# The delta rule of a four-layer kernel in chunks of 128 tokens instead of 64

## What is computed

```python
C = 64                                        # chunk; N = 512 // C chunks
dec = cumsum(decay, within each chunk)
L_mask = exp(where(lower, dec_i - dec_j, -inf))
M = strict_lower(wk_beta @ wk.T * L_mask)
A = solve_triangular(eye(C) + M, eye(C))      # inverse of a unit lower triangle
v, wk_cumdecay = A @ v, A @ (wk_beta * exp(dec))
def step(S, chunk):                           # over the chunks, in order
    v_new = v_i - wkcd_i @ S
    o_i = (rk_i * exp(dec_i)) @ S + lower(rk_i @ wk_i.T * L_i) @ v_new
    S = S * exp(dec_i[-1]) + (wk_i * exp(dec_i[-1] - dec_i)).T @ v_new
```

## Time and profile before

| | before |
|---|---|
| median of 3 runs | 4818.0 us |
| span of the profiled execution | 4823.4 us |
| PE busy (matmul) | 4293.7 us, 89% |
| PE weight loads | 3431.0 us, 71% |
| DVE busy | 3207.6 us, 67% |
| ACT busy | 2619.0 us, 54% |
| POOL busy | 2413.5 us, 50% |

### The profile page before, as it was taken

The page is one execution under the profiler, slowest core; times in us unless marked ns, Lnnn a source line. Parts: engine busy times, 40 slices in busy tenths (PEclk is TensorE's granted clock), DMA queues, the critical chain, the costliest instruction groups (busy, mean ns, idle before and its releaser), DMA issues. The chain is left out here.

```text
span 4823.4 us, 167277 instructions
## 1 busy us (share of the span) xinstructions
PE 4293.7 (89%) x70890; PEld 3431.0 (71%) x70890; DVE 3207.6 (67%) x5446; ACT 2619.0 (54%) x4310; POOL 2413.5 (50%) x1965
## 2 busy tenths in 40 slices
PE   6997999999999999999999999999997768568767
PEld 5885777777777777777777777777774558457556
DVE  4445777777777777777778777777774553563553
ACT  2232566666566666566665666665664435445544
POOL 2123665566665656555656556566551255225034
PEclk9777999999999999999999999999998868768877
DMA  0000322222222222222222222232220111221022
GB/s 25 0 0 30 91 65 64 68 81 69 63 71 80 68 66 67 63 81 72 65 64 80 71 67 64 63 79 64 68 67 18 59 26 40 54 67 45 16 72 66
DMA packets 214409, 281.74 MB, mean 58 GB/s; under 512 B 59070, under 2 KB 103908, under 8 KB 212932
## 3 DMA queue, kind: packets, MB, share of 16 engines
q1 hardware_dynamic: 199940, 249.75, 19.5%
q0 software_dynamic: 9536, 19.55, 1.5%
q10 hardware_dynamic: 4224, 2.10, 0.2%
HBM read 54.88 MB, written 18.28 MB: 15 GB/s over the span
## 5 line engine op out<-in xcount | busy, mean ns | idle before, releaser
L1696 POOL TENSOR_TENSOR local_normed<-local_rot,local_sines 128x512 f32<-128x512 f32 x768 | 953.7, 1276 | 810.6 <-PE local_bank L1421 806.1
L1706 POOL TENSOR_TENSOR local_normed<-local_normed,local_inv_norm 128x1024 f32<-128x1024 f32 x384 | 733.1, 1930 | 278.3 <-ACT local_inv_norm L1596 278.3
L1773 DVE TENSOR_TENSOR local_rot<-local_bank,local_table 128x1024 f32<-128x1024 f32 x384 | 470.3, 1225 | 404.0 <-ACT local_squares L1577 397.4
L1341 PE MATMUL local_bank<-local_wqkv_hi,local_ys_hi 128*128 128x512 f32 x1152 | 494.8, 430 | 28.9 <-issue 17.4
L1572 ACT COPY local_v_tile<-local_bank 128x1024 f32<-128x1024 f32 x192 | 195.0, 1016 | 541.4 <-PE local_bank L1343 541.4
L1773 DVE TENSOR_TENSOR local_sines<-local_bank,local_table 128x1024 f32<-128x1024 f32 x384 | 466.4, 1215 | 0.0
L1779 DVE TENSOR_REDUCE local_norm<-local_squares 128x16 f32<-128x1024 f32 x384 | 464.1, 1209 | 0.0
L1343 PE MATMUL local_bank<-local_wqkv_hi,local_ys_lo 128*128 128x512 f32 x1152 | 458.1, 398 | 0.0
L1342 PE MATMUL local_bank<-local_wqkv_lo,local_ys_hi 128*128 128x512 f32 x1152 | 455.6, 395 | 0.0
L1577 ACT ACTIVATE local_squares<-local_bank 128x1024 f32<-128x1024 f32 x384 | 396.6, 1033 | 77.9 <-PE local_bank L1343 77.9
L1760 DVE TENSOR_REDUCE local_top<-local_bank 128x16 f32<-128x1024 f32 x192 | 234.8, 1223 | 244.9 <-PE local_bank L1369 244.5
(11 more groups left out here) (408 smaller groups left out, 9101.1 us busy)
## 6 DMA issues: line engine op xcount, KB each, us to landing
local_vals<-local_v_tile SPq DMA_DIRECT2D x1152, 130.0 KB
local_vals<-local_v_tile SPq DMA_DIRECT2D x672, 65.0 KB
local_stage<-in_L_ffn_Wqkv SPq DMA_DIRECT2D x6, 1536.0 KB
moe_w<-in_L_ffn_W SPq DMA_DIRECT2D x3, 2048.0 KB, 9.9
x_rows<-moe_rows SPq DMA_DIRECT2D x24, 256.0 KB, 4.9
moe_w<-y_rows SPq DMA_DIRECT2D x24, 256.0 KB, 5.5
local_wo<-in_L_ffn_Wo SPq DMA_DIRECT2D x6, 512.0 KB
moe_taken<-x_rows,moe_take POOLq DMA_INDIRECT x149
```

Of the source, the lines that this page charges most:

```text
L1341: nc.tensor.matmul(out, hi, wqkv_hi[:, d0:d1], start=True, stop=False)
L1696: last = nc.gpsimd.tensor_tensor(of_heads(normed, a)[:, :, to], of_heads(rot, a)[:, :, to], of_heads(sines, a)[:, :, of], ALU.add)
L1706: nc.gpsimd.tensor_tensor(of_heads(normed, a), of_heads(normed, a), inv_norm[:, a * HEADS:(a + 1) * HEADS].unsqueeze(2).to_broadcast([P, H ...
L1773: last = nc.vector.tensor_tensor(of_heads(out, a), src, table[:, m % TILES, row, :].unsqueeze(1).to_broadcast([P, HEADS, HD]), ALU.mult)
```

## The change

The chunk becomes the whole tile of 128 tokens. The doubling stage gets a seventh level, which joins blocks of 64 to 128; the tables `until`, `within`, `ceiling` and `corner` are made for whole tiles, and `ends` goes with its products and its load, since a chunk's end value is now the total by `within`. The state loop has four steps of whole tiles, and in it the product for the state's update is issued ahead of the output half.

```diff
-    PAIRS, CHUNK, LEVELS = SEQS // 2, 64, 6
-    CHUNKS = TOKENS // CHUNK
+    PAIRS, LEVELS = SEQS // 2, 7
...
-        carry = ph.sb("carry", [P, 2, CHUNKS])
+        carry = ph.sb("carry", [P, 2, TILES])
...
-        LOADS = 16 * 12
+        LOADS = 16 * 11
...
                         nc.tensor.matmul(bank[i][1][:, 16:20], until[:], sm["decay"][:, i], start=True, stop=True)
-                        nc.tensor.matmul(bank[i][1][:, 20:24], within[:], sm["decay"][:, i], start=True, stop=True)
-                        for t in range(TILES):
-                            last = nc.tensor.matmul(bank[i][1][:, 24 + 2 * t:26 + 2 * t], sm["decay"][:, i, t:t + 1].to_broadcast([P, P]), ends[:],
-                                                    start=True, stop=True)
-                        done(last, "decs_done", i)
+                        done(nc.tensor.matmul(bank[i][1][:, 20:24], within[:], sm["decay"][:, i], start=True, stop=True), "decs_done", i)
...
-                    for c in range(CHUNKS):
-                        t, rows, own = c // 2, slice(CHUNK * (c % 2), CHUNK * (c % 2) + CHUNK), slice(c * CHUNK, (c + 1) * CHUNK)
+                    for t in range(TILES):
+                        own = cols[t]
                         for i in range(2):
...
-                            wait(pe, pair, "state_ready", i, c + 1)
-                            done(nc.tensor.matmul(bank[i][2][rows, 0:P], big["wkcd_t"][:, i, own], state[:, i], start=True, stop=True), "vs_done", i)
+                            wait(pe, pair, "state_ready", i, t + 1)
+                            done(nc.tensor.matmul(bank[i][2][:, 0:P], big["wkcd_t"][:, i, own], state[:, i], start=True, stop=True), "vs_done", i)
                             nc.tensor.matmul(bank[i][3][:, own], state[:, i], big["rkd_t"][:, i, own], start=True, stop=False)
                         for i in range(2):
...
-                            last = nc.tensor.matmul(bank[i][3][:, own], big["v_new"][rows, i, cols[t]], big["attn_t"][rows, i, own], start=False, stop=True)
-                            if c == CHUNKS - 1:
+                            done(nc.tensor.matmul(bank[i][0][:, 0:P], big["wkdw"][:, i, own], big["v_new"][:, i, own], start=True, stop=True), "update_done", i)
+                            last = nc.tensor.matmul(bank[i][3][:, own], big["v_new"][:, i, own], big["attn_t"][:, i, own], start=False, stop=True)
+                            if t == TILES - 1:
                                 done(last, "o_done", i)
-                            done(nc.tensor.matmul(bank[i][0][:, 0:P], big["wkdw"][rows, i, cols[t]], big["v_new"][rows, i, cols[t]], start=True, stop=True), "update_done", i)
...
-                        done(nc.scalar.activation(carry[:, i], bank[i][1][:, 24:32], ACT.Exp), "carry_ready", i)
+                        done(nc.scalar.activation(carry[:, i], bank[i][1][:, 20:24], ACT.Exp), "carry_ready", i)
...
-                            done(nc.vector.tensor_tensor(big["v_new"][rows, i, cols[t]], big["vp"][rows, i, cols[t]], bank[i][2][rows, 0:P], ALU.subtract), "v_new_ready", i)
+                            done(nc.vector.tensor_tensor(big["v_new"][:, i, cols[t]], big["vp"][:, i, cols[t]], bank[i][2][:, 0:P], ALU.subtract), "v_new_ready", i)
...
-    c["until"] = (same & (j <= i)).astype(f)
-    c["within"] = same.astype(f)
-    c["ends"] = (j // 64 == np.arange(2)[None]).astype(f)
-    c["ceiling"] = np.where(same & (j <= i), f(-NEVER), f(NEVER))
-    c["corner"] = np.stack([((i >> b) % 2 == 1) & (j >> b == (i >> b) - 1) for b in range(6)], 1).astype(f)
+    c["until"] = (j <= i).astype(f)
+    c["within"] = np.ones((P, P), f)
+    c["ceiling"] = np.where(j <= i, f(-NEVER), f(NEVER))
+    c["corner"] = np.stack([((i >> b) % 2 == 1) & (j >> b == (i >> b) - 1) for b in range(7)], 1).astype(f)
```

More of the change, by code:

```diff
@@ L1924, in body @@
         within = ph.sb("within", [P, P])
-        ends = ph.sb("ends", [P, 2])
         ceiling = ph.sb("ceiling", [P, P])
@@ L1950, in body @@
         count.update(t1_done=LEVELS, t1_ready=LEVELS - 1, u_done=LEVELS - 2, ut_done=LEVELS - 1, inv_ready=LEVELS, inv_t_ready=LEVELS, off_ready=LEVELS,
-                     vs_done=CHUNKS, update_done=CHUNKS, v_new_ready=CHUNKS, state_ready=CHUNKS + 1)
+                     vs_done=TILES, update_done=TILES, v_new_ready=TILES, state_ready=TILES + 1)
         q = {k: [ph.sem(f"{k}{i}") for i in range(2)] for k in ("t1_done", "t1_ready", "u_done", "ut_done", "inv_ready", "inv_t_ready", "off_ready",
@@ L2002, in _ @@
                                  (dt_bias[:], w["dt_bias"].partition_broadcast(P)), (a_log[:], w["A_log"].partition_broadcast(P)),
-                                 (until[:], w["until"]), (within[:], w["within"]), (ends[:], w["ends"]), (ceiling[:], w["ceiling"]),
+                                 (until[:], w["until"]), (within[:], w["within"]), (ceiling[:], w["ceiling"]),
                                  (corner[:], w["corner"])):
@@ L2091, in _ @@
                         products(i, 1, lambda t: big["wkbd"][:, i, cols[t]], lambda t: big["inv_t"][:, i, cols[t]], "wkcd_done")
[L2092 to L2093 removed]
+                    for t in range(TILES):
+                        own = cols[t]
                         for i in range(2):
[L2095 removed]
+                            if t == 0:
                                 wait(pe, pair, "wkcd_ready", i)
                                 wait(pe, pair, "vp_ready", i)
[L2098 to L2099 removed]
+                            wait(pe, pair, "state_ready", i, t + 1)
+                            done(nc.tensor.matmul(bank[i][2][:, 0:P], big["wkcd_t"][:, i, own], state[:, i], start=True, stop=True), "vs_done", i)
                             nc.tensor.matmul(bank[i][3][:, own], state[:, i], big["rkd_t"][:, i, own], start=True, stop=False)
                         for i in range(2):
[L2102 to L2103 removed]
+                            wait(pe, pair, "v_new_ready", i, t + 1)
+                            if t == 0:
                                 wait(pe, pair, "wkdw_ready", i)
[L2105 to L2106 removed]
+                            done(nc.tensor.matmul(bank[i][0][:, 0:P], big["wkdw"][:, i, own], big["v_new"][:, i, own], start=True, stop=True), "update_done", i)
+                            last = nc.tensor.matmul(bank[i][3][:, own], big["v_new"][:, i, own], big["attn_t"][:, i, own], start=False, stop=True)
+                            if t == TILES - 1:
                                 done(last, "o_done", i)
[L2108 removed]
                     for i in range(2):
@@ L2265, in _ @@
                         dve.sem_inc(q["inv_ready"][i], 1)
-                    for c in range(CHUNKS):
-                        t, rows = c // 2, slice(CHUNK * (c % 2), CHUNK * (c % 2) + CHUNK)
+                    for t in range(TILES):
                         for i in range(2):
-                            if c == 0:
+                            if t == 0:
                                 wait(dve, pair, "vp_ready", i)
-                            wait(dve, pair, "vs_done", i, c + 1)
-                            done(nc.vector.tensor_tensor(big["v_new"][rows, i, cols[t]], big["vp"][rows, i, cols[t]], bank[i][2][rows, 0:P], ALU.subtract), "v_new_ready", i)
+                            wait(dve, pair, "vs_done", i, t + 1)
+                            done(nc.vector.tensor_tensor(big["v_new"][:, i, cols[t]], big["vp"][:, i, cols[t]], bank[i][2][:, 0:P], ALU.subtract), "v_new_ready", i)
                         for i in range(2):
-                            wait(dve, pair, "update_done", i, c + 1)
-                            wait(dve, pair, "state_ready", i, c + 1)
-                            done(nc.vector.scalar_tensor_tensor(state[:, i], state[:, i], carry[:, i, c:c + 1], bank[i][0][:, 0:P], ALU.mult, ALU.add), "state_ready", i)
+                            wait(dve, pair, "update_done", i, t + 1)
+                            wait(dve, pair, "state_ready", i, t + 1)
+                            done(nc.vector.scalar_tensor_tensor(state[:, i], state[:, i], carry[:, i, t:t + 1], bank[i][0][:, 0:P], ALU.mult, ALU.add), "state_ready", i)
                     for i in range(2):
@@ L2352, in build_program @@
         delta_rule_phase(nc, g, "delta", of("L0_attn", "W_write", "W_gate", "W_out", "W_beta", "W_alpha", "dt_bias", "A_log")
-                         | {n: a[n] for n in ("until", "within", "ends", "ceiling", "corner")})
+                         | {n: a[n] for n in ("until", "within", "ceiling", "corner")})
         local_transformer_phase(nc, g, "local", of("L0_ffn", "Wqkv", "q_scale", "k_scale", "Wo", "ln_g", "ln_b", "W1", "b1", "W2", "b2")
```

## The result

The changed kernel takes 4731.66 us (median of 4 runs, 4723.96 to 4736.09) beside 4816.93 us (4 runs) for the kernel before on the same chip: a ratio of 0.9815 on record, with a 95% interval of 0.9802 to 0.9828 (these two medians alone give 0.9823; the ratios below are those on record too). The forecast was 4726, the range 4708 to 4762. The profiled execution spans 4734.2 us, 89.2 less than the one before.

The account below looks back on a forecast made before the run. PE (TensorE) was taken to bound the delta phase, its state loop the dearest stage. Terms -95.5 - 4.0 - 2.5 - 11.2 + 21.6 = -91.6 us gave 4732 from the profiled 4823.4, carried to 4726 us; range 4708 to 4762.

Parts of the forecast that it names:

- The loop: State loop: four whole-tile steps of 1.87 us at full clock, 32.4 us over four rounds instead of 127.86, -95.5 us.
- The chain: In a loop step: state product, DVE's difference, update product, DVE's state update, then the next step, 1.87 us in all.
- the first rival: State loop: the clock falls as before, giving 4757 us if at once, 4738 if after 5.4 us; chance 0.10.
- The cause: State loop: PE's 0.33 us wait before a weight load comes from changing tile form and goes with one form.
- Behind the loop: Output products after the loop start at full clock instead of half: -1.0 us a round, -4.0 in all.
- The next round's start: Start of the fourth round runs at full clock like the second's if the loop ends so: -2.5 us.
- The chunk-end products: Decay stage: these products go, PE being the bound, and "wk" is copied 2.8 us earlier a round: -11.2 us.
- The further 12 us: Decay stage: range allowance of -12 us if the clock also stays up there, about 3 us a round.
- The seventh level: Doubling stage: one more period of 5.41 us a round at full clock, +21.6 us.
- the third rival: Levels: PE never gets its clock back ahead of them, levels of 10.8 us, 4908 us in total; chance 0.03.
- POOL's masks: Doubling stage: two more masked tiles a round on POOL, covered; without that cover 2.6 us a round.
- a sign against itself: Forecast is wrong if the delta phase is less than 80 us shorter or another phase changes by more than a few microseconds.

Follow-up runs that it names:

- The run with one whole product: Kernel before, eight steps kept, with only the state product taking all 128 columns of its tile: 4765.6 us beside 4821.38, ratio 0.9891.
- Eight whole steps: Changed kernel with its loop run over each tile twice, so eight steps of whole products (output of another recursion): 4767.46 us in one run.
- the second profile: Profile of the changed kernel run once more, unchanged, beside others on one chip: 4725.63 us, ratio 0.9815.
- The slowed run: Changed kernel with each tile taken twice and DVE's difference cut into pieces, five first, then eight: steps of 2.14 and 2.41 us; no total given.
- the split state product: Changed kernel with each state product issued as two products of 64 weight columns, arithmetic unchanged: 4735.31 us in one run.

## Why the prediction was right

Step by step, as the prediction put it:

- *The loop*, -95.5 forecast, 32.81 - 127.86 = -95.05 measured. A step was put at 1.87 us and takes 1.82 (185.14 to 186.96); the loop 8.1 and takes 8.19, since the first step is longer: 2.33 us instead of 2.12. The chain was put a little too long: DVE's state update follows its product by 0.43 us (186.07 to 186.50) and not by 0.57, so that PE's stream of eight products sets the step. The clock is 1.00 throughout: the first rival falls, also for twice the length. The run with one whole product splits the term: about 40 of the 95 us (10 in each of four loops) come from the clock that no longer falls, and some 14 from the waits at the change of form. Eight whole steps take 65.00 us in the four loops, so that of the rest some 9 go to the changes that were left and the new order, and 32 to having half as many steps.
- *The cause.* The prediction laid the wait to the change of form, and the run with one whole product shows it: three changes fewer, 0.43 us less a step, with more arithmetic. The Trainium skill, TensorEngine Tiling (Array Packing), section Key Properties, says that changing the tiling mode drains the engine. By that rule every change pays, of rows or of columns; the traces agree, at 0.14 to 0.20 us a change at full clock.
- *Behind the loop*, -4.0 forecast: 3.23 instead of 4.15, -0.92 a round or -3.7; the first y follows after 1.19 us (191.00 to 192.19), forecast 1.15.
- *The next round's start*, -2.5 forecast: the four starts fall by 2.85 together in the first profile, but by 1.3 in the second, where the clock falls inside the third and fourth start (7.06 us at 0.66, 7.73 at 0.60). That the clock of the loop carries over to the start thus held in one profile and not in the other.
- *The chunk-end products*, -11.2 forecast: decays and keys fall from 51.00 us over four rounds to 38.26, -12.7, of which the products are 10.5. "wk" was to be copied 2.8 us earlier; from the first product of the decays to that copy it was 9.63 us (152.60 to 162.23) and is 6.81 (130.02 to 136.83, rows below). That this agrees so well is in part luck, since its two parts miss by 0.4 us in opposite directions: the keys' turn comes 5.51 us behind the first product (at 135.53) and not 5.11, and the copy 1.30 behind the turn and not 1.70. PE was not the only bound: in this round it waits 0.31 us for the second sequence's decays (132.80), which the prediction had ruled out. The further 12 us that the range allowed for a clock that stays up into the decays would not have come either (9.40 at 0.98, 9.41 at 0.56 in the second profile).
- *The seventh level*, +21.6 forecast, 4 x 5.41 measured, at 1.00: the third rival falls. POOL's masks, forecast to be hidden, still end long before the loop:

```profile
132.80 0.50 PEld L2041 LDWEIGHTS delta_bank<-delta_decay,delta_until 128*128 128x128 f32 x2 [0.31 <-DVE delta_decay L2219]
...
136.83 0.57 ACT L2120 COPY delta_wk<-delta_bank 128x512 f32<-128x512 f32 x1
...
144.58 16.86 POOL L2180 TENSOR_TENSOR delta_off_t<-delta_m_t,delta_corner 128x512 f32<-128x512 f32 x13 [0.51 <-DVE delta_m_t L2240]
...
164.37 1.07 POOL L2186 TENSOR_TENSOR delta_wkdw<-delta_wk,delta_e_to_end 128x512 f32<-128x512 f32 x1
```

- *The sum.* -91.6 forecast and -92.3 at the end of the phase. The total missed by 5.7 us and, in the second measurement, by 0.4; the last section shows that this is no term of the sum. The prediction named as a sign against itself that another phase changes by more than a few microseconds; the local phase did, by 5.4 us in the first profile, but not in the second (3258.15 beside 3258.30). A microsecond saved in the phase is one saved in the total only to within such differences.

On the clock, the Trainium skill, TensorE: Matmul & The Clock Gate, section HAM oscillation, lays its fall to idle PE. The loop before does not agree: at 0.50 PE was busy 22.41 of 22.41 us, though the ends of matmuls are modelled, so that short stops at a change of form may be hidden in that. The slowed run is no test of the rule, since its waits are short.

## What to carry to other kernels

If a chain of small matmuls is slow, look at the distance between starts and at "issue" ahead of weight loads, and then for a change between whole and half columns or rows of the loaded weights: here a product with twice the columns was cheaper than the half, because its neighbours were whole, and with the shorter step the granted clock held. Cost each removed stage at the clock of its own stretch and check what follows it for the same clock; a stretch at half clock need not be bound by it, as the decays show. Judge a change of a few microseconds by the phase that it touches, not by the total.

## What the runs showed of the hardware that was not expected

**A phase that nothing changed moves by more than the miss.** The local phase behind the delta phase has the same code in all runs. Its first load and the first load of the phase behind it, in the first profile of the changed kernel and in the second:

```profile
341.74 0.33 SPq L1275 DMA_DIRECT2D local_base<-in_rotary  x1
...
3605.43 0.35 SPq L670 DMA_DIRECT2D causal_wq<-in_L_attn_wq  x1
```
```profile
343.36 0.33 SPq L1275 DMA_DIRECT2D local_base<-in_rotary  x1
...
3601.51 0.35 SPq L670 DMA_DIRECT2D causal_wq<-in_L_attn_wq  x1
```

It lasted 3263.69 us in one and 3258.15 in the other, 3258.30 before, and between 3253.63 and 3265.23 over the 14 profiles. That is why the delta phase won 92.3 us and the first profiled span only 89.2: the local phase took 5.4 more, and what lies behind it 2.3 less. The profiled execution with the chunk-end products put back was even 4.8 us shorter than the changed kernel's (4729.4), with a delta phase 10.7 longer (305.06) and a local phase of 3253.63.

**Half the columns of two products run side by side.** The two halves of the split state product start at the same 188.15, and the pair costs what one half did before (0.36).
